# Block 0 of a cross-attention and expert layer: first loads on ScalarE's queue, row transposes ahead of values, squares of the expert weights regrouped

## The chip, the cores and the metric

The kernel runs on one core of a Trainium2 chip. The metric is the device time of one execution in microseconds (us), the median of several runs. Engines: TensorE (PE, with its weight loads PEld), VectorE (DVE), ScalarE (ACT), GpSimd (POOL) and SyncE (SP, which issues most transfers). A name with q behind it (SPq, ACTq) is the engine's sequencer, here when it issues a transfer.

## What is computed

```
x = x + attn(layernorm(x), ctx)   # 8 sequences of 256 tokens, 512 wide; 32 query heads of 16, 8 key/value groups
                                  #   q = ln(x) Wq', k = ctx Wk', v = ctx Wv', softmax(q k'/4) v, Wfc', + bfc
x = x + ffn(layernorm(x))         # 8 experts of width 352, top 2 of them within the 2 best of 4 groups,
                                  #   softmax gate, silu(g) * u, and a shared expert of width 704
```

All inputs are float32. The kernel splits float32 operands of its large products into two float16 parts (a high part and the rest), scaled by powers of two that it derives from maxima or sums of squares of the data, and takes three float16 products for one float32 product.

## The kernel before

The 2048 tokens are taken in four **blocks** of 512 tokens (`BLOCKS = 4`, `BT = 512`), each of four tiles of 128 tokens (`TPB = 4`). The first phase, to which the change belongs, ends about 103 us after the start. For each block n it computes keys (`project_k`, PE line 1087, 4 pairs of float32 matmuls into bank 0), values (`project_v(n, a)`, line 1092, one tile a at a time into bank 5), the transposed normalised rows (`x_transpose(n, a)`, line 1156, into four banks) and the queries (`project_q(n, m)`, line 1111, four groups m of 12 float16 matmuls). Later phases are attention (lines 1205, 1219, 1135 on PE, exponentials at ACT line 948), the output projection with the second layernorm, and the experts (PE lines 1377 and 1391).

Around these matmuls:

- **DVE** makes the layernorm of a block (`norm_block`, from line 1573 to 1586; for blocks 2 and 3 the last step, subtract and multiply, is POOL's, line 714), the largest absolute key (`k_top`, line 1600), the reduction of that over partitions (`top_of_all`, lines 1606 and 1608, between two small PE transposes, `top_transpose` at line 1120 and `top_back` at line 1124), the power-of-two scales (`top_scale`, lines 1614 to 1623), and the second float16 parts: of the transposed rows (`xT_rest`, line 1642), of the query weights (`wq_rest`, line 1658), of keys and queries (`cut_rest(n, l)`, line 1636; l = 0 is the keys, 1 to 4 the query groups). In blocks 2 and 3 it also reduces score maxima (line 1592) for fills that PE makes between halves of a query group.
- **ACT** makes the first float16 parts (`xT_first` line 883, `wq_first` line 889, `cut_first` line 861), copies the values out of their bank (`v_out`, line 895), takes the square root of a block's variance (`std_block`, line 866), squares the query weights to find their scale (line 901) and squares the gate and up weights of the ten expert matrices, in 20 halves (`square_half(h)`, line 871), each with its sum in one column.
- **SP** issues the loads and stores in one order. It loads block 0's rows (`load_x_block(0)`, line 408), then for each quarter k of the contraction the key/value weights and the context (lines 400 and 401), then the query weights in one transfer (line 418). It waits for the last quarter of the context, then issues rows and context of block 1, halves 0 and 1 of the expert weights (line 414), rows of block 2, and halves 2 and 3. In the loop over blocks it stores each pair of parts as soon as its second part is there (`store_parts`, line 432) and behind each store loads the half that is four further on (`load_half`), which waits until the half in that buffer has been squared. The parts are in three buffers, so `cut_first` number i waits until the store of number i - 3 has landed.

The order on each engine is written out by hand. In block 0 PE runs keys, three tiles of values, the transposes for both scales, the last tile of values, both `top_back`s, the four row transposes, then the queries. In blocks 1 to 3 it runs keys, row transposes, two tiles of values, then waits for the block's `k_top`, and goes on with `top_transpose`, two tiles of values, `top_back`, queries.

Of the kernel before, what the change touches and what calls it, by code (L numbers as in the profile page):

```python
# [31 lines left out]
D = 512  # L32
# [48 lines left out]
def build(nc, x, ctxT, wqT, wkvT, wfcT, bfc, gwT, wgu, wdn, out):  # L81
# [17 lines left out]
    with ExitStack() as ctx:  # L99
# [141 lines left out]
        def small(at, n):  # L241
# [10 lines left out]
        rstds, warm = [rstd[:], small(408, TPB)], small(416, TPB)  # L252
        WQ = BLOCKS
# [107 lines left out]
            sem("soft_in"), sem("soft_exp"), sem("sel_done"), sem("pre_ready"), sem("slots_done"), sem("offs_done"))  # L361
        iotas, hot_ready, table_ready, toks_done = sem("iotas"), sem("hot_ready"), sem("table_ready"), sem("toks_done")
# [12 lines left out]
        out_st, OUT_SEEN = x_ld + [w_q], (32, 16, 16, 16)  # L375
# [15 lines left out]
        def _(sp):  # L391
# [24 lines left out]
            load_x_block(0)  # L416
            load_ctx(0)
            sp.dma_start(wq_sb, wqT).then_inc(w_q, 16)
# [430 lines left out]
        def _(act):  # L849

            for stored in parts_st + lnt_stored:
                act.sem_inc(stored, FREE)
# [39 lines left out]
            def v_out(n):  # L892
# [7 lines left out]
            act.wait_ge(w_q, 16)  # L900
            nc.scalar.activation(wq_words, wq_sb.rearrange("p k n -> p (k n)"), ACT.Square,
                                 accum_out=kq_max[:, WQ:WQ + 1]).then_inc(wq_square, 1)
            for n in range(BLOCKS):
                if n == 0:
                    xT_first(0, 0)
                    act.wait_ge(kq_scaled, 1)
                    wq_first(0)
                    for a in range(1, TPB):
                        xT_first(0, a)
# [7 lines left out]
                if n == BLOCKS - 1:  # L917
                    neg_max_rows(0, 0, 0)
                if n < 2:
                    std_block(1 + n)  # L920
                square_half(KQ * n)
                for l in range(1, KQ):
                    cut_first(n, l)
                    if n < BLOCKS - 1:
                        square_half(KQ * n + l)
                    elif l < KQ - 1:
                        for h in ((16, 17), (18,), (19,))[l - 1]:
                            square_half(h)
# [122 lines left out]
            act.wait_ge(soft_in, 1)  # L1051
# [25 lines left out]
        def _(pe):  # L1077
# [82 lines left out]
            for n in range(BLOCKS):  # L1160
                last = n == BLOCKS - 1
                project_k(n)
                if n == 0:
                    for a in range(3):
                        project_v(n, a)
# [3 lines left out]
                    pe.wait_ge(kq_max_done, 1)  # L1169
                    top_transpose(0, bank[4])  # L1170
                    project_v(n, 3)
                    top_back(0, bank[3])
                    top_back(1, bank[4])
                    for a in range(TPB):
                        x_transpose(n, a)
                else:
# [6 lines left out]
                    project_v(n, 0)  # L1183
                    project_v(n, 1)
                    pe.wait_ge(kq_max_done, n + 1)
                    pe.wait_ge(rest_done, n * KQ + KQ)
                    top_transpose(n, bank[4])
                    project_v(n, 2)
                    project_v(n, 3)
                    top_back(n + 1, bank[4])  # L1190
                pe.wait_ge(xT_free, (n + 1) * TPB)
# [53 lines left out]
            pe.wait_ge(nm_in[0], 32)  # L1245
            for f in range(2):
                score_fill(0, f)
            for G in range(UNITS * UG):
# [12 lines left out]
                if G + 1 < UNITS * UG:  # L1261
                    if j == UG - 1:
                        pe.wait_ge(nm_in[(u + 1) % 4], (u + 1) // 4 * 32 + 32)
                    score_fill(G + 1, 0)
# [269 lines left out]
        def _(dve):  # L1534
# [110 lines left out]
            def neg_max_part(v, par, at=7):  # L1645
                dve.wait_ge(mxt_ready, v + 1)
                if v >= 2:
                    dve.wait_ge(nm_in[(v - 2) % 4], (v - 2) // 4 * 32 + 32)
# [13 lines left out]
            for n in range(BLOCKS):  # L1662
                v = n - 2
                k_top(n)
                if n == 0:
                    top_of_all(0, bank[3])
                    top_of_all(1, bank[4])
                    top_scale(0, WQ, bank[3])
                    top_scale(1, 0, bank[4])
                    exp_factor(0)  # L1670
                    xT_rest(0, 0)
                    wq_rest(0)
                    for a in range(1, TPB):
                        xT_rest(0, a)
                    wq_rest(1)
                    cut_rest(0, 0)
                    wq_rest(2)
                    wq_rest(3)
                else:
                    if n == BLOCKS - 1:  # L1680
                        neg_max_part(0, 0, at=3)
                    for a in range(TPB):
                        xT_rest(n, a)
                    top_of_all(n + 1, bank[4])
# [577 lines left out]
```

## Time and profile before

| | us |
|---|---|
| median of 3 runs | 849.8 (845.85 to 851.85) |
| the profiled execution, whole | 843.12 |
| its span, first to last instruction | 841.4 |
| PE busy in the span | 801.7 |
| DVE busy | 597.5 |
| ACT busy | 446.2 |
| POOL busy | 269.5 |
| mean granted TensorE clock | 0.991 of full |

The span is 1.7 us shorter than the execution's own time; the rest lies before the first and behind the last instruction. Busy shares are means over the whole kernel; the timeline rows further down show single stretches of it, with the start and the length of each group of instructions, and in brackets how long the engine had been idle before and what released it.

### The profile page before, as it was taken

How to read it: one execution, taken by the hardware profiler on the slowest of the kernel's cores; microseconds unless marked ns; L12 is line 12 of the kernel's file. 1: busy time of each engine (PE TensorE's matmuls, PEld its weight loads, DVE VectorE, ACT ScalarE, POOL GpSimd, SP SyncE). 2: the span in 40 equal slices, each digit the busy share in tenths (PEclk: the TensorE clock that was granted, in tenths of full speed). 3: DMA queues.
4: the chain of work that ended last, by engine and by line, in shares of the span. 5: the costliest groups of instructions: out<-in, count | busy, mean ns of one | idle time of the engine just before them, and what ended most of it. 6: DMA issues, size and time to landing. Idle time of an engine off the chain costs nothing.

```text
span 841.4 us, 17104 instructions
## 1 busy us (share of the span) xinstructions
PE 801.7 (95%) x5498; PEld 447.1 (53%) x5499; DVE 597.5 (71%) x1224; ACT 446.2 (53%) x876; POOL 269.5 (32%) x224
## 2 busy tenths in 40 slices
PE   5999999999999989999889999999999999999996
PEld 3553433333433346666545656666666666666663
DVE  4767789999999769896786665555555555546656
ACT  2665689999999835565335633333333333333332
POOL 2361029999953015661000111111111111032321
PEclk9999989999999999999999999999999999999999
DMA  8996755555457989976711222322322322156673
GB/s 314 365 363 216 229 196 181 162 191 189 156 149 229 324 300 326 372 248 219 282 51 63 88 85 78 97 78 75 100 75 77 97 75 82 56 177 202 186 212 125
DMA packets 68675, 149.08 MB, mean 177 GB/s; under 512 B 10704, under 2 KB 24528, under 8 KB 67984
## 3 DMA queue, kind: packets, MB, share of 16 engines
q1 hardware_dynamic: 57436, 106.99, 36.9%
q0 software_dynamic: 11120, 41.43, 15.9%
q8 instruction: 29, 0.48, 0.2%
q14 instruction: 22, 0.18, 0.1%
q10 hardware_dynamic: 68, 0.02, 0.0%
HBM read 105.40 MB, written 42.73 MB: 176 GB/s over the span
## 4 chain that ended last, share of the span: by engine, by line
PE 74%; DVE 12%; DMA 5%; ACT 5%; issue 3%; SPq 1%; DVEq 0%; ACTq 0%
PE psum L1377 26%; PE psum L1391 15%; PE psum L1219 8%; PE psum L1205 6%; PE psum L1135 4%; PE psum L1305 3%; PE psum L1367 3%; DMA sb_weights<-attn_dram 2%; PE psum L1111 2%; PE psum L1471 2%; PE psum L1236 2%; DMA sb_weights<-in_wdn 2%; DMA sb_weights<-in_wqT 1%; DVE sb_stats L1573 1%; DVE sb_rows L1592 1%
## 5 line engine op out<-in xcount | busy, mean ns | idle before, releaser
L1377 PE MATMUL psum<-sb_weights,sb_rows 128*128 (+1 forms) x1608 | 263.2, 314 | 0.6 <-issue 0.6
L1377 PEld LDWEIGHTS psum<-sb_weights,sb_rows 128*128 128x128 f16 x1608 | 157.5, 98 | 78.3 <-issue 0.8
L948 ACT ACTIVATE sb_weights<-psum,sb_rows 128x512 f32<-128x512 f32 x256 | 158.2, 684 | 16.9 <-PE psum L1205 15.0
L1391 PE MATMUL psum<-sb_weights,sb_hT 128*128 (+1 forms) x639 | 150.6, 381 | 4.7 <-DVE sb_hT L1853 4.7
L1592 DVE TENSOR_REDUCE sb_rows<-psum 128x4 f32<-128x1024 f32 x128 | 149.9, 1214 | 4.3 <-PE psum L1135 4.3
L825 POOL DMA_INDIRECT sb_rows<-xn_rows,sb_slot_tok x39 | 38.1, 978 | 267.8 <-PE psum L1471 204.9
L1018 ACT ACTIVATE psum<-sb_h 128x352 f32<-128x352 f32 x71 | 33.2, 468 | 144.4 <-DVE sb_h L1835 144.4
L1391 PEld LDWEIGHTS psum<-sb_weights,sb_hT 128*128 128x128 f16 x639 | 62.0, 98 | 72.9 <-DVE sb_hT L1853 7.3
L1030 ACT CAST sb_hT<-psum 128x384 f16<-128x384 f32 x71 | 33.9, 478 | 113.6 <-PE psum L1367 113.2
L1205 PE MATMUL psum<-sb_weights 50*128 50x512 f16 x256 | 90.1, 391 | 3.0 <-ACT sb_weights L948 2.6
L1853 DVE TENSOR_TENSOR sb_hT<-psum,sb_hT 128x384 f16<-128x384 f32 x71 | 39.3, 554 | 72.5 <-ACT sb_hT L1030 72.5
L1219 PE MATMUL psum<-sb_weights 128*32 128x256 f32 x1024 | 82.9, 396 | 0.0
L1135 PE MATMUL psum<-sb_weights 48*128 48x256 f16 x512 | 73.0, 275 | 0.8 <-DVE sb_rows L1592 0.8
L1305 PE MATMUL psum<-sb_weights 128*128 128x512 f32 x128 | 57.7, 594 | 0.3 <-ACT sb_weights L958 0.3
L843 POOL DMA_INDIRECT sb_weights<-slot_y,sb_p_i x32 | 32.2, 1005 | 80.3 <-DMA out<-sb_weights 42.5
L1205 PEld LDWEIGHTS psum<-sb_weights 50*128 50x128 f16 x256 | 23.6, 93 | 63.3 <-ACT sb_weights L948 59.1
L1023 ACT ACTIVATE sb_h<-sb_h,sb_h_scale_i 128x352 f32<-128x352 f32 x71 | 41.8, 588 | 15.7 <-DVE sb_h_scale_i L1841 15.7
L1111 PE MATMUL psum<-sb_weights 128*128 128x512 f16 x192 | 44.6, 380 | 2.9 <-DVE sb_weights L1642 2.9
L734 POOL TENSOR_TENSOR sb_weights<-sb_weights,sb_w_scale_i 128x1408 f32<-128x1408 f32 x15 | 38.5, 2570 | 26.6 <-ACT sb_weights L990 25.8
L1841 DVE TENSOR_SCALAR sb_h_scale_i<-sb_h_sum 128x1 int32<-128x1 int32 x71 | 10.9, 154 | 46.7 <-ACT psum L1018 46.7
L744 POOL TENSOR_TENSOR sb_weights<-sb_weights 128x1408 f16<-128x1408 f32 x15 | 43.0, 2864 | 1.2
L1367 PE MATMUL psum<-sb_ident,sb_h 128*128 128x128 f32 x213 | 35.6, 277 | 2.5 <-ACT sb_h L1023 2.3
(254 smaller groups left out, 1126.5 us busy)
## 6 DMA issues: line engine op xcount, KB each, us to landing
sb_weights<-in_wgu SPq DMA_DIRECT2D x20, 704.0 KB, 6.1
sb_weights<-in_wgu POOLq DMA_DIRECT2D x20, 704.0 KB, 5.5
sb_weights<-in_wdn SPq DMA_DIRECT2D x17, 768.0 KB, 6.4
slot_y<-sb_rows SPq DMA_DIRECT2D x39, 256.0 KB, 2.0
sb_weights<-q_parts SPq DMA_DIRECT2D x96, 64.0 KB, 2.3
x_dram<-sb_rows SPq DMA_DIRECT2D x24, 256.0 KB, 2.5
sb_weights<-in_x SPq DMA_DIRECT2D x4, 1024.0 KB, 7.5
q_parts<-sb_weights SPq DMA_DIRECT2D x16, 256.0 KB, 4.4
```

Of the source, the lines that this page charges most:

```text
L744: nc.gpsimd.tensor_tensor(low, stage, high, ALU.subtract).then_inc(gu_cut, 1)
L948: nc.scalar.activation(probs[G % 2][:, kt, pair * 512:(pair + 1) * 512], bank[4 + f % 2], ACT.Exp, scale=exp_scale[:, n:n + 1]).then_inc(e ...
L1023: nc.scalar.activation(h_sb[par][:, 0:F], h_sb[par][:, 0:F], ACT.Copy, scale=h_scale[:, par:par + 1]).then_inc(h_done, 1)
L1111: mm = nc.tensor.matmul(bank[Q_BANKS[n][m]], wq16[:, wp, k, m * P:(m + 1) * P], xnT[n % 2][:, xp, k, :], start=(k == 0 and i == 0), stop=( ...
L1135: mm = nc.tensor.matmul(bank[banks[qt] + side][:, h * SEQ:(h + 1) * SEQ], q_st[s][lo:hi, g, h, b * SEQ + qt * P:b * SEQ + (qt + 1) * P], k ...
L1205: nc.tensor.matmul(bank[4 + side].rearrange("p (h t) -> p h t", h=HH), k_st[s][lo:hi, g, b * SEQ + kt * P:b * SEQ + (kt + 1) * P], q_st[s] ...
L1219: mm = nc.tensor.matmul(bank[6][VW * c:VW * (c + 1), 0:SEQ], v_now, probs[G % 2][:, kt, c * SEQ:(c + 1) * SEQ], start=(kt == 0), stop=(kt ...
L1305: mm = nc.tensor.matmul(bank[2 + s][:], oT[s][:, k, :], wfc_sb[:, k, :], start=(k == 0), stop=(k == KD - 1))
L1367: tr = nc.tensor.transpose(bank[HT_BANK][:, j * P:(j + 1) * P], h_sb[par][:, j * P:(j + 1) * P], ident[:])
L1377: mm = nc.tensor.matmul(bank[GU_BANKS[par][which]][:, 0:F], x_T[:, xp * D + k * P:xp * D + (k + 1) * P], gu(wp, k, which), start=(k == 0 a ...
L1391: mm = nc.tensor.matmul(bank[Y_BANKS[par]][:], hT[par][:, hp, j, :], dn(wp, j), start=(j == 0 and n == 0), stop=(j == NF - 1 and n == 2))
L1592: nc.vector.tensor_reduce(to[:, :, j // UB, :, j % UB, qt], psum[:, banks[qt] * 512:(banks[qt] + 2) * 512] .rearrange("p (a h k) -> p a h ...
```

## The change

Three things change, all of them in the first phase.

1. ACT issues block 0's rows as its first instruction and behind them the query weights in four transfers of 256 KB, one per quarter of the contraction. SP starts with the context and no longer issues these. The query weights are squared quarter by quarter, each with its own sum in one column of `wq_squares`, and DVE adds the four sums.
2. In block 0 PE makes the row transposes ahead of the values. `k_top(0)` and the scale of the keys come behind the scale of the query weights on DVE. In all blocks PE now waits for `k_top` before any values, then runs `top_transpose`, two tiles of values, `top_back` (in block 0 behind the fourth tile), two tiles of values. DVE takes `top_of_all` ahead of the block's last `xT_rest`.
3. The 20 squares of the expert weights are grouped (2, 1, 1, 1, 0) per block: two behind the keys' first part and ahead of the next block's square root, one behind each of the next three `cut_first`, none behind the last.

Some waits on shared semaphores get an offset, because two semaphores serve a second purpose.

```diff
@@ SP
-            load_x_block(0)
             load_ctx(0)
-            sp.dma_start(wq_sb, wqT).then_inc(w_q, 16)
             sp.wait_ge(c_first[KD - 1], 32)
@@ ACT
+            act.dma_start(x_in[0], x_blocks[0]).then_inc(x_ld[0], 16)
+            for k in range(KD):
+                act.dma_start(wq_sb[:, k, :], wqT[:, k, :]).then_inc(wq_ld[k], 16)
...
             std_block(0)
-            act.wait_ge(w_q, 16)
-            nc.scalar.activation(wq_words, wq_sb.rearrange("p k n -> p (k n)"), ACT.Square,
-                                 accum_out=kq_max[:, WQ:WQ + 1]).then_inc(wq_square, 1)
+            for k in range(KD):
+                act.wait_ge(wq_ld[k], 16)
+                nc.scalar.activation(wq_words[:, k * D:(k + 1) * D], wq_sb[:, k, :], ACT.Square,
+                                     accum_out=wq_squares[:, k:k + 1]).then_inc(wq_squared, 1)
+            SQUARES = (2, 1, 1, 1, 0)
             for n in range(BLOCKS):
                 if n == 0:
-                    xT_first(0, 0)
+                    for a in range(2):
+                        xT_first(0, a)
                     act.wait_ge(kq_scaled, 1)
                     wq_first(0)
-                    for a in range(1, TPB):
+                    for a in range(2, TPB):
                         xT_first(0, a)
...
+                for h in range(SQUARES[0]):
+                    square_half(KQ * n + h)
                 if n < 2:
                     std_block(1 + n)
-                square_half(KQ * n)
                 for l in range(1, KQ):
                     cut_first(n, l)
-                    if n < BLOCKS - 1:
-                        square_half(KQ * n + l)
-                    elif l < KQ - 1:
-                        for h in ((16, 17), (18,), (19,))[l - 1]:
-                            square_half(h)
+                    for h in range(sum(SQUARES[:l]), sum(SQUARES[:l + 1])):
+                        square_half(KQ * n + h)
@@ PE
                 project_k(n)
                 if n == 0:
-                    for a in range(3):
-                        project_v(n, a)
                     pe.wait_ge(consts, 2)
                     pe.wait_ge(wq_square, 1)
                     top_transpose(WQ, bank[3])
-                    pe.wait_ge(kq_max_done, 1)
-                    top_transpose(0, bank[4])
-                    project_v(n, 3)
+                    for a in range(2):
+                        x_transpose(0, a)
                     top_back(0, bank[3])
-                    top_back(1, bank[4])
-                    for a in range(TPB):
-                        x_transpose(n, a)
+                    for a in range(2, TPB):
+                        x_transpose(0, a)
                 else:
...
                     pe.wait_ge(v_free, n + 1)
-                    project_v(n, 0)
-                    project_v(n, 1)
-                    pe.wait_ge(kq_max_done, n + 1)
                     pe.wait_ge(rest_done, n * KQ + KQ)
-                    top_transpose(n, bank[4])
-                    project_v(n, 2)
-                    project_v(n, 3)
+                pe.wait_ge(kq_max_done, n + 1)
+                top_transpose(n, bank[4])
+                project_v(n, 0)
+                project_v(n, 1)
+                if n > 0:
                     top_back(n + 1, bank[4])
+                project_v(n, 2)
+                project_v(n, 3)
+                if n == 0:
+                    top_back(1, bank[4])
@@ DVE
-                k_top(n)
                 if n == 0:
+                    dve.wait_ge(wq_squared, KD)
+                    nc.vector.tensor_reduce(kq_max[:, WQ:WQ + 1], wq_squares, AX.X, ALU.add).then_inc(wq_square, 1)
+                    k_top(0)
                     top_of_all(0, bank[3])
-                    top_of_all(1, bank[4])
                     top_scale(0, WQ, bank[3])
-                    top_scale(1, 0, bank[4])
-                    exp_factor(0)
                     xT_rest(0, 0)
                     wq_rest(0)
                     for a in range(1, TPB):
                         xT_rest(0, a)
+                    top_of_all(1, bank[4])
                     wq_rest(1)
+                    top_scale(1, 0, bank[4])
+                    exp_factor(0)
                     cut_rest(0, 0)
                     wq_rest(2)
                     wq_rest(3)
                 else:
+                    k_top(n)
...
-                    for a in range(TPB):
+                    for a in range(3):
                         xT_rest(n, a)
                     top_of_all(n + 1, bank[4])
+                    xT_rest(n, 3)
```

## Rows read from the trace of the kernel before

**Rows 1.** The page: busy time (us, share, instructions), and shares of the last chain

```profile
PE 801.7 (95%) x5498; PEld 447.1 (53%) x5499; DVE 597.5 (71%) x1224; ACT 446.2 (53%) x876; POOL 269.5 (32%) x224
...
PE 74%; DVE 12%; DMA 5%; ACT 5%; issue 3%; SPq 1%; DVEq 0%; ACTq 0%
```

**Rows 2.** Stretches of 3 us: busy us by engine, clock, DMA share, GB/s

```profile
3.00:6.00 3.00, 0.00 (x0) 0.00 (x0) 0.00 (x0) 0.15 (x1) 2.88 (x5) 1.00 1.05 376
...
33.00:36.00 3.00, 3.00 (x9) 1.43 (x8) 1.40 (x3) 3.00 (x5) 2.84 (x4) 1.00 0.86 281
...
63.00:66.00 3.00, 1.44 (x11) 0.97 (x10) 2.59 (x9) 1.18 (x3) 3.00 (x2) 1.00 1.01 385
```

**Rows 3.** Timeline, block 0: start, length, engine, line, operation, idle before

```profile
0.81 0.46 SPq L408 DMA_DIRECT2D sb_weights<-in_x  x1
...
6.10 2.47 DVE L1573 BATCH_NORM_STATS2 sb_stats<-sb_weights 128x6 f32<-128x512 f32 x4 [6.10 <-DMA sb_weights<-in_x]
...
9.23 0.21 ACT L866 ACTIVATE sb_std<-sb_var_e 128x4 f32<-128x4 f32 x1 [6.08 <-DVE sb_var_e L1579]
...
10.47 1.92 DVE L1586 TENSOR_SCALAR sb_weights<-sb_weights,sb_mv,sb_rstd 128x512 f32<-128x512 f32 x4
...
11.77 0.38 SPq L408 DMA_DIRECT2D sb_weights<-in_x  x1
...
14.23 1.91 ACT L901 ACTIVATE sb_weights<-sb_weights 128x2048 f32<-128x2048 f32 x1 [4.80 <-DMA sb_weights<-in_wqT]
...
16.05 0.19 ACT L901 ACTIVATION_READ_ACCUMULATOR sb_weights<-sb_weights 128x1 f32 x1
...
17.84 0.16 DVE L1614 TENSOR_SCALAR sb_rows<-psum 128x1 f32<-128x1 f32 x1 [0.17 <-PE psum L1124]
...
22.75 10.54 PE L1111 MATMUL psum<-sb_weights 128*128 128x512 f16 x48 [2.91 <-DVE sb_weights L1642]
...
26.14 2.46 DVE L1573 BATCH_NORM_STATS2 sb_stats<-sb_weights 128x6 f32<-128x512 f32 x4
```

**Rows 4.** Timeline, head of block 1, columns as in rows 3

```profile
37.49 0.60 ACT L861 ACTIVATE sb_weights<-psum 128x512 f16<-128x512 f32 x1 [1.15 <-DMA q_parts<-sb_weights]
37.99 1.37 ACT L871 ACTIVATE sb_weights<-sb_weights 128x1408 f32<-128x1408 f32 x1
...
38.73 0.68 DVE L1600 TENSOR_REDUCE sb_rows<-psum 128x1 f32<-128x512 f32 x1
...
39.97 2.48 DVE L1642 SCALAR_TENSOR_TENSOR sb_weights<-psum,sb_weights 128x512 f16<-128x512 f32 x4 [0.55 <-ACT sb_weights L883]
...
40.19 1.95 PE L1092 MATMUL psum<-sb_weights 128*128 128x128 f32 x16
...
43.09 3.20 PE L1111 MATMUL psum<-sb_weights 128*128 128x512 f16 x14
```

**Rows 5.** Timeline, end of block 1 and head of block 2, same columns

```profile
53.04 2.46 DVE L1573 BATCH_NORM_STATS2 sb_stats<-sb_weights 128x6 f32<-128x512 f32 x4
...
62.16 2.48 DVE L1642 SCALAR_TENSOR_TENSOR sb_weights<-psum,sb_weights 128x512 f16<-128x512 f32 x4 [0.56 <-ACT sb_weights L883]
...
65.43 1.47 PE L1111 MATMUL psum<-sb_weights 128*128 128x512 f16 x6
```

**Rows 6.** Timeline, head of block 3, same columns

```profile
87.00 1.95 PE L1092 MATMUL psum<-sb_weights 128*128 128x128 f32 x16
...
89.03 1.47 PE L1111 MATMUL psum<-sb_weights 128*128 128x512 f16 x6
...
89.87 0.69 ACT L861 ACTIVATE sb_weights<-psum,sb_rows 128x512 f16<-128x512 f32 x1 [0.30 <-DVEq L1624]
```

**Rows 7.** Stretches of 1 us at attention's start, columns as in rows 2

```profile
104.00:105.00 1.00, 0.26 (x1) 0.09 (x1) 1.00 (x2) 1.00 (x2) 0.00 (x0) 1.00 0.34 98
...
106.00:107.00 1.00, 1.00 (x6) 0.30 (x5) 0.38 (x1) 1.00 (x2) 0.00 (x0) 0.62 0.33 103
...
112.00:113.00 1.00, 1.00 (x8) 0.37 (x6) 0.27 (x1) 0.24 (x1) 0.00 (x0) 0.50 0.30 74
```

More of the change, by code:

```diff
@@ L252, in build @@
         rstds, warm = [rstd[:], small(408, TPB)], small(416, TPB)
+        wq_squares = small(420, KD)
         WQ = BLOCKS
@@ L361, in build @@
             sem("soft_in"), sem("soft_exp"), sem("sel_done"), sem("pre_ready"), sem("slots_done"), sem("offs_done"))
+        wq_ld, NM_SEEN = nm_in, 16
+        wq_squared, SOFT_SEEN = soft_in, KD
         iotas, hot_ready, table_ready, toks_done = sem("iotas"), sem("hot_ready"), sem("table_ready"), sem("toks_done")
@@ L374, in build @@
         out_done = sem("out_done")
-        out_st, OUT_SEEN = x_ld + [w_q], (32, 16, 16, 16)
+        out_st, OUT_SEEN = x_ld + [w_q], (32, 16, 16, 0)
         B0, C0 = PA, PA + PB
@@ L1049, in _ @@
             hidden_scale(1, 1)
-            act.wait_ge(soft_in, 1)
+            act.wait_ge(soft_in, 1 + SOFT_SEEN)
             nc.scalar.activation(score, score, ACT.Exp).then_inc(soft_exp, 1)
@@ L1244, in _ @@
             pe.wait_ge(v_free, BLOCKS + 1)
-            pe.wait_ge(nm_in[0], 32)
+            pe.wait_ge(nm_in[0], 32 + NM_SEEN)
             for f in range(2):
@@ L1262, in _ @@
                     if j == UG - 1:
-                        pe.wait_ge(nm_in[(u + 1) % 4], (u + 1) // 4 * 32 + 32)
+                        pe.wait_ge(nm_in[(u + 1) % 4], (u + 1) // 4 * 32 + (32 + NM_SEEN))
                     score_fill(G + 1, 0)
@@ L1647, in neg_max_part @@
                 if v >= 2:
-                    dve.wait_ge(nm_in[(v - 2) % 4], (v - 2) // 4 * 32 + 32)
+                    dve.wait_ge(nm_in[(v - 2) % 4], (v - 2) // 4 * 32 + (32 + NM_SEEN))
                 nc.vector.tensor_scalar(nm[par][:, 0, :], bank[at][0:NM, MXT:MXT + P], -1.0 / ONE, None,
```

## The prediction

> **What bounds the kernel now.** I read the page first: PE is busy for 95% of the span and carries 74% of the chain that ended last [rows 1]. That share is a mean; the change touches only the first phase, about 105 of 841 us, so the question is what sets the pace there. The table by stretches of 3 us says that PE is far from full in places: in 63 to 66 it works 1.44 of 3 us. It says too that the DMA engines are full (share 1.00 and more) from 3 us on and still are at 63 to 66, with dips such as 0.86 at 33 to 36 [rows 2]. Then I read the timeline for the head of each block, because there PE changes from one kind of matmul to the next through a chain over ACT and DVE.
>
> Block 0 [rows 3]: the rows, issued at 0.81, land at 6.10; the last context quarter has landed at 11.77 (SP's next load is released then); the query weights are there at 14.23, and their square is read out by 16.24. The first scale is read by DVE at 17.84, PE starts queries at 22.75, and DVE reaches block 1's layernorm at 26.14. Block 1 [rows 4]: DVE's `k_top` stands at 38.73, the first `xT_rest` at 39.97, queries start at 43.09. Block 2 [rows 5]: 62.16 and 65.43. Block 3 [rows 6]: queries at 89.03, straight behind the values; PE alone sets it.
>
> **The loads.** The same 3.67 MB (rows 1.05, key/value weights 0.52, context 1.05, query weights 1.05) go over DMA engines that are already full [rows 2]. A second issuer brings them no bandwidth, so the last of them lands at about 14.2 as before, and what is gained by ACT issuing query weights early is taken from the context or the rows. The sum takes nothing here. The rows now share with context from the start. Their landing is bounded by 6.1 (as if alone) and 11.8 (together with all context) [rows 3]; no row shows the sharing, so I take the middle, 8.9. In its own sentences: the Trainium skill, "DMA: Bandwidth & Descriptors", section "Queues, rings and completion order", says that each DMA engine goes round between the queues packet by packet. By that rule 1.05 MB of context pass beside the rows, 2.8 us at 376 GB/s, and the rows land at 8.9; were the queues served in order of issue they would land at 6.1, and the end would come out about 0.1 us earlier than below, since then the last quarter of the weights bounds the squares. No row of the kernel before has two such queues side by side, so the trace neither agrees nor disagrees.
>
> **The squares of the query weights.** ACT takes the root first. The root now starts 3.13 us behind the rows' landing (9.23 less 6.10) and takes 0.21 [rows 3]: 8.9 + 3.3 = 12.2. A square of 2048 columns takes 1.91 and one of 1408 takes 1.37 [rows 3, 4], 0.84 ns a column, so 512 columns take 0.61, and 0.19 for each read-out: 0.80. Four of them: 12.2 + 3.2 = 15.4 (or 14.2 + 0.8 = 15.0, if the last quarter bounds). DVE adds the four sums, about 0.2; its layernorm is done by then (8.9 + 6.29 = 15.2, from 6.10 to 12.39). At 15.65 `k_top(0)`, which used to be hidden, stands in the chain with 0.68 [rows 4]; then the reduction over partitions and the way through PE, 0.65 (43.09 less 42.45, where the block 1 chain does the same) [rows 4]. The first scale is read at 17.0 instead of 17.84: **0.8 us gained**.
>
> **From there to block 1.** Before, DVE took 8.30 us from the first scale to the next layernorm [rows 3]. Now the keys' scale comes after all `xT_rest` and one `wq_rest`; `cut_first(0, 0)` on ACT (0.7) can't start before it and used to be covered by DVE's other work, and `wq_rest(0)` waits about 0.25 for a first part that itself waits for the scale. I add 1.0: 9.3, so layernorm 1 starts at 26.3 (+0.15). The gain of 0.8 is spent. PE's order lets values (four tiles, 3.9 by [rows 4]) run under DVE's parts; queries start behind DVE's scale and its five second parts (4.35 us), `top_of_all` and `top_back` (0.95 together), at 17.0 + 5.3 = 22.3, 0.45 earlier, and this has no taker, because PE then waits for DVE in block 1. SP: two ahead of one, halves 4 and 5 are asked for some 4 us earlier; the engines are full, so what is in the queue ahead of a store stays about the same. The store that releases `cut_first(0, 4)` at 37.49 [rows 4] is issued behind DVE's layernorm 1, and I leave it there (+0.1). The bound upward: half 4 lands so late that its square, now ahead of `cut_first(0, 4)`, pushes it by up to 0.8.
>
> **Head of block 1 (the term that costs).** What the regrouping frees: ACT's square of 1.37 and its 0.19 no longer stand between `cut_first(0, 4)` and `xT_first(1, 0)`. DVE idled 0.55 for it [rows 4]. That is the gain, 0.5, since `k_top` and `cut_rest` keep DVE busy anyway. What the wait costs: PE now stands until `k_top` is done (39.4 to 39.6) and only then starts values that it had made from about 38.2 on (two tiles ahead of 40.19), under `k_top`. From there: `top_transpose` 0.25, two tiles 1.95 [rows 4], `top_back` 0.35 to 0.5 later (three `xT_rest` and `top_of_all` are 2.4 to 2.5), two tiles 1.95: 4.65 us from `k_top`'s end to queries, against 43.09 less 39.41 = 3.68 before. Queries start at 39.6 + 4.65 = 44.25, **1.15 later** than before. Behind that wait on PE stand the values, `top_back` and the queries; behind the values stands `v_out` on ACT, and behind it `cut_first(1, 0)`, so layernorm 2 starts some 0.9 later.
>
> **Block 2.** The regrouping gives part of that back in block 1: the squares fall into ACT's idle time ahead of the root, so ACT is late by 0.1 to 0.2 at layernorm 3 (53.2 against 53.04 [rows 5]), not by 0.9. The last `cut_first` stands where it was, and DVE's idle 0.56 ahead of the first `xT_rest` (62.16) [rows 5] goes: `k_top` ends at about 61.75. Plus 4.65: queries at 66.4 against 65.43, 1.0 later, of which 0.75 reaches the second fill, since the keys' scale is ready earlier.
>
> **Block 3.** All is shifted by 0.75. The head is PE's own work [rows 6] and `k_top` has been long done, so the reordering costs nothing; its cover is DVE's idle time. The keys' scale, on which ACT waited 0.30 at 89.87 [rows 6], is ready before: 0.25 back. **Sum: +1.15 and +1.0 are not added, the second contains the first; +0.75 - 0.25 = +0.5 us** at the start of attention, and behind it everything starts by the same semaphores. The profiled execution goes from 843.1 to 843.6; the median of 849.8 is 6.7 above that execution, so I forecast 850.3.
>
> **Rivals.**
> *The gain arrives.* If DVE gets its first scale earlier and the wait on `k_top` hides (values finish before `top_back` anyway), the 0.8 of the head and 0.5 of each of two heads come through: -1.8, so 848.0. For it: DVE's two idle gaps are real [rows 4, 5]. Against: 1.95 us of values lose their cover in two blocks.
> *Rows late.* This one ends slower than before. Layernorm 0 ends 6.29 behind the rows. From a landing at 9.4 on, it and not the squares sets the first scale, and each further us costs one. With the context (11.8) that is 2.4, with the last weights (14.2) 4.8: 852.7 to 855.1. For it: the DMA engines are full [rows 2]. Against: the rows are first in ACT's queue.
> *A colder clock.* At 104 to 105 PE is busy for 0.26 of 1 us; the granted clock is 0.62 at 106 to 107 and 0.50, that is 1.2 GHz, until 113 [rows 7]: 6.6 us at half, 3.3 lost where PE sets the pace. The longer wait at the heads of blocks 1 and 2 could bring the same there, 853.6; or the shift could spare the one at 106, 847. Against: in block 0, PE stands 2.91 us before 22.75 [rows 3], longer than any new wait, with full clock behind it. In sentences of its own: the Trainium skill, "TensorE: Matmul & The Clock Gate", Part 1, says that the clock is halved after idle time and returns after sustained work, and that when this falls varies from run to run. By it the fall after 104 fits, while block 0's wait without one doesn't show it; it gives the same 853.6.
> *It does nothing.* Full DMA engines pin the landings on which the heads wait; 849.8. It differs from my forecast by less than can be measured.
>
> **How the numbers follow.** Forecast 0.45 (its own range 849 to 852), the gain arrives 0.2, rows late 0.12, clock 0.08, nothing 0.15. The runs of before lie 4 below to 2 above their median, which is wider than most of these terms, and about 1% (8.5 us) is what a measurement of this kernel can tell from no change. Low end: 848.0 less 3.5; high end: 855.1 plus 1. Over 1% faster would need 8.5 us in a phase where PE's summed waits at the heads are smaller: 0.03. Over 1% slower needs late rows and a fallen clock together: 0.04.
>
> **What would show it.** Right: first scale read near 17.0; layernorm 1 within 0.5 of 26.14; no idle DVE between `k_top(1)` and the first `xT_rest`; `k_top`'s end to queries 4.65 in blocks 1 and 2; block 3 unchanged but for the earlier `cut_first`; attention starting 0.5 later. Wrong: the rows landing past 9.4, the context's last quarter much past 11.8 (it holds back block 1's loads), `cut_first(0, 4)` behind half 4's landing, or a granted clock of 0.5 before 100 us.

## The result and the profile after

| | before | changed |
|---|---|---|
| median of 20 runs, us | 848.7 (843.9 to 853.7) | 852.6 (848.6 to 855.4) |
| ratio, 95% interval | | 1.0042 (1.0024 to 1.0060) |
| profiled execution, span | 841.4 | 846.8 |
| first exponential of attention, us after the start | 104.0 | 106.35 |

The changed kernel is slower by 0.4%, some 3.6 us. I had forecast +0.5 us. The first exponential (ACT) marks the end of the phase that was changed; up to there the profiled execution has lost 2.35 us. The timeline of the changed kernel, columns as in rows 3; these rows answer to those of [rows 3]:

```profile
7.18 2.47 DVE L1577 BATCH_NORM_STATS2 sb_stats<-sb_weights 128x6 f32<-128x512 f32 x4 [7.18 <-DMA sb_weights<-in_x]
...
11.99 5.28 PE L1092 MATMUL psum<-sb_weights 128*128 128x512 f32 x6 [1.52 <-DMA sb_weights<-in_ctxT]
...
14.70 0.16 DVE L1670 TENSOR_REDUCE sb_rows<-sb_rows 128x1 f32<-128x4 f32 x1 [1.23 <-ACT sb_weights L906]
...
15.09 0.39 SPq L411 DMA_DIRECT2D sb_weights<-in_x  x1
...
17.30 0.69 DVE L1604 TENSOR_REDUCE sb_rows<-psum 128x1 f32<-128x512 f32 x1 [2.45 <-PE psum L1092]
...
18.74 0.16 DVE L1618 TENSOR_SCALAR sb_rows<-psum 128x1 f32<-128x1 f32 x1 [0.31 <-PE psum L1129]
...
23.56 10.53 PE L1116 MATMUL psum<-sb_weights 128*128 128x512 f16 x48
...
27.46 2.47 DVE L1577 BATCH_NORM_STATS2 sb_stats<-sb_weights 128x6 f32<-128x512 f32 x4
```

The rows land at 7.18 (6.10 before). The query weights are squared and summed at 14.86, against 16.24 before: that part does what it says. But the context's last quarter lands at 15.09 instead of 11.77 (SP's next load of rows is released by it). PE's keys end at 17.3 (line 1092 is `project_k` in the changed kernel), `k_top(0)` (line 1604) waits 2.45 for them, and the first scale is read at 18.74, 0.9 later than before, not 0.8 earlier. The table by stretches of 2 us (columns as in rows 2) shows a second effect. First the kernel before:

```profile
12.00:14.00 2.00, 2.00 (x14) 1.52 (x14) 1.08 (x2) 0.00 (x0) 0.00 (x0) 1.00 0.67 229
14.00:16.00 2.00, 1.60 (x15) 1.41 (x13) 0.00 (x0) 1.77 (x1) 0.00 (x0) 1.00 1.07 407
16.00:18.00 2.00, 1.62 (x13) 1.49 (x14) 1.07 (x5) 0.23 (x2) 0.00 (x0) 1.00 1.01 380
```

Then the changed kernel, in which the DMA engines stand still (share 0.07) just where they used to be full:

```profile
12.00:14.00 2.00, 2.00 (x2) 0.49 (x2) 1.47 (x4) 1.15 (x5) 0.00 (x0) 1.00 0.68 256
14.00:16.00 2.00, 1.90 (x3) 0.84 (x3) 0.16 (x1) 0.67 (x2) 0.00 (x0) 1.00 0.07 26
16.00:18.00 2.00, 2.00 (x12) 1.31 (x10) 0.69 (x2) 0.15 (x1) 0.00 (x0) 1.00 0.68 224
```

Before, the query weights were behind the context in the one queue and kept the engines busy while SP waited for the context and issued the next loads. Now both queues drain together, and nothing is queued until SP is released at 15.09. The next loads in SP's queue are asked for about 3 us later, and at the head of block 1 ACT runs late behind transfers (ACT's timeline; compare [rows 4]):

```profile
37.20 0.60 ACT L865 ACTIVATE sb_weights<-psum 128x512 f16<-128x512 f32 x1 [1.70 <-DMA k_parts<-sb_weights]
38.84 1.38 ACT L875 ACTIVATE sb_weights<-sb_weights 128x1408 f32<-128x1408 f32 x1 [1.04 <-DMA sb_weights<-in_wgu]
...
40.21 0.58 ACT L865 ACTIVATE sb_weights<-psum 128x512 f16<-128x512 f32 x1
40.69 2.05 ACT L887 ACTIVATE sb_weights<-psum 128x512 f16<-128x512 f32 x4
```

A `cut_first` waits 1.70 for the store of the keys' parts (issued at 26.25, landed 10.9 us later, behind the loads), the square behind it 1.04 for half 4, and `cut_first(0, 4)` comes at 40.21 instead of 37.49. The two waits themselves are not made by the late context: they stand in e2 below too, nearly as long, but 2.9 us earlier. Queries of block 1 start at 46.43 (43.09 before), of block 2 at 68.30 (65.43), of block 3 at 91.53 (89.03).

### The profile page after: what moved, and what is told of

Read it like the earlier page. It is cut to its first block, busy times and chain, and to the rows that moved or that the text cites. A ratio compares the mean times of both kernels' runs of the same rounds, so it can differ in the third digit from the quotient of the medians.

```text
span 846.8 us, 17114 instructions
## 1 busy us (share of the span) xinstructions
PE 802.4 (95%) x5498; PEld 446.7 (53%) x5499; DVE 597.0 (71%) x1225; ACT 447.8 (53%) x882; POOL 269.4 (32%) x224
## 3 DMA queue, kind: packets, MB, share of 16 engines
q0 software_dynamic: 11120, 41.43, 15.5%
## 4 chain that ended last, share of the span: by engine, by line
PE 74%; DVE 11%; DMA 6%; ACT 4%; issue 3%; SPq 1%; another core or an unknown queue 0%; ACTq 0%; DVEq 0%
PE psum L1381 26%; PE psum L1395 14%; PE psum L1223 7%; PE psum L1209 6%; PE psum L1140 4%; PE psum L1309 4%; PE psum L1116 3%; PE psum L1371 3%; PE psum L1475 2%; PE psum L1240 2%; DMA sb_weights<-in_wdn 2%; DMA sb_weights<-attn_dram 2%; DMA sb_weights<-in_wgu 1%; DMA sb_weights<-in_ctxT 1%; PE psum L1097 1%
## 5 line engine op out<-in xcount | busy, mean ns | idle before, releaser
L953 ACT ACTIVATE sb_weights<-psum,sb_rows 128x512 f32<-128x512 f32 x256 | 158.5, 684 | 17.0 <-PE psum L1209 15.1
L1861 DVE TENSOR_TENSOR sb_hT<-psum,sb_hT 128x384 f16<-128x384 f32 x71 | 39.3, 554 | 70.8 <-ACT sb_hT L1035 68.3
L1849 DVE TENSOR_SCALAR sb_h_scale_i<-sb_h_sum 128x1 int32<-128x1 int32 x71 | 10.9, 154 | 46.7 <-ACT psum L1023 46.7
```

The costliest lines, as they stand in the source:

```text
L953: nc.scalar.activation(probs[G % 2][:, kt, pair * 512:(pair + 1) * 512], bank[4 + f % 2], ACT.Exp, scale=exp_scale[:, n:n + 1]).then_inc(e ...
```

## The experiments

"First exp" is the first exponential in the profiled execution; it moves by what the first phase gains or loses, and nothing behind that phase blurs it. It is still the mark of a single execution: two kernels were traced twice, and their marks differ by 0.8 (e11 and e12) and 1.2 us (changed and e13, where the clock fell once in the second). So a difference of 2 us between two rows is clear of this spread, and tenths are not. Each ratio is against runs of the kernel before on the same chip, with its 95% interval.

| kernel | context's last quarter | queries of blocks 1, 2, 3 start | first exp | ratio |
|---|---|---|---|---|
| before | 11.8 | 43.1, 65.4, 89.0 | 104.00 | |
| changed | 15.1 | 46.4, 68.3, 91.5 | 106.35 | 1.0042 (1.0024 to 1.0060) |
| e1 loads only | 15.0 | 48.0, 70.3, 93.9 | 108.86 | 1.0027 (0.9999 to 1.0056) |
| e2 changed, loads back | 11.9 | 43.5, 66.0, 89.3 | 104.09 | 0.9991 (0.9961 to 1.0021) |
| e3 changed, SP doesn't wait | | 43.7, 67.1, 90.6 | 105.45 | 0.9994 (0.9970 to 1.0018) |
| e4 squares only | 11.9 | 43.9, 64.5, 87.8 | 102.77 | 0.9987 (0.9955 to 1.0018) |
| e5 later blocks' order only | 11.8 | 43.7, 67.8, 91.4 | 106.20 | 1.0011 (0.9979 to 1.0042) |
| e6 changed, that order back | 15.0 | 45.1, 65.5, 89.1 | 104.07 | 0.9997 (0.9973 to 1.0022) |
| e7 loads and order back | 11.8 | 42.2, 63.7, 86.8 | 101.79 | 0.9970 (0.9938 to 1.0001) |
| e8 as e7, SP doesn't wait | | 41.5, 63.7, 88.4 | 103.38 | 0.9956 (0.9925 to 0.9988) |
| e10 changed, only the rows on ACT | 10.8 | 42.3, 64.5, 87.9 | 102.72 | 0.9996 (0.9963 to 1.0029) |
| e11 as e10, order back | 10.7 | 40.6, 62.0, 85.2 | 100.13 | 0.9898 (0.9861 to 0.9936) |
| e12, e11 again | 10.5 | 40.8, 62.4, 86.0 | 100.95 | 0.9959 (0.9933 to 0.9986) |
| e13, changed again | 15.1 | 47.8, 69.5, 92.8 | 107.59 | 1.0051 (1.0027 to 1.0074) |

**e1, the loads alone.** The kernel before with the loads and the quartered square (the square's lines are left out here):

```diff
-            load_x_block(0)
             load_ctx(0)
-            sp.dma_start(wq_sb, wqT).then_inc(w_q, 16)
...
+            act.dma_start(x_in[0], x_blocks[0]).then_inc(x_ld[0], 16)
+            for k in range(KD):
+                act.dma_start(wq_sb[:, k, :], wqT[:, k, :]).then_inc(wq_ld[k], 16)
```

> The kernel before with only the loads and the quartered square of the query weights taken over (ACT issues block 0's rows and the query weights); the orders on PE and the grouping of the expert squares stay. Theory A (the hole in the transfers): the context's last quarter lands near 15.1 instead of 11.8, the next loads are issued 3.3 us later and the DMA engines idle between 13 and 17; queries of block 1 start at 45 to 46 instead of 43.1, the first exponential comes at 105.5 to 106.5 instead of 104.0, time +1.5 to +2.5 us. Theory B (PE's wait on the largest key costs, the loads don't): first exponential at 104 +- 0.3, time unchanged.

The context is late as in the changed kernel, and the phase loses 4.9 us, more than expected. The granted clock was 0.52 and 0.62 from 28 to 32 in this execution, in the middle of block 0's queries, so a part of the 4.9 may be that. But 4.05 us were already lost at the first scale (21.89 against 17.84), before the clock fell: in the old order of block 0 three tiles of values stand on PE between the keys and the transposes for both scales, so late keys push the first scale by more than in the changed kernel. A loss from the loads is shown; for the changed kernel its size is better read from the pairs below.

**e2, the changed kernel with the loads back on SP** (query weights in quarters behind the context).

```diff
+            load_x_block(0)
             load_ctx(0)
+            for k in range(KD):
+                sp.dma_start(wq_sb[:, k, :], wqT[:, k, :]).then_inc(wq_ld[k], 16)
...
-            act.dma_start(x_in[0], x_blocks[0]).then_inc(x_ld[0], 16)
-            for k in range(KD):
-                act.dma_start(wq_sb[:, k, :], wqT[:, k, :]).then_inc(wq_ld[k], 16)
```

> The changed kernel with its loads on SP again in the old order (rows, context, query weights, the last still in quarters); the new orders and the new grouping stay. Theory A: the context has landed at 11.8, no idle DMA engines, queries of block 1 near 44.2, first exponential at 104.3 to 104.8, time near +0.5 us over the kernel before. Theory B: the head of block 1 still costs 2 us and more, first exponential near 106.

Its timeline, DVE and SP, then ACT at the head of block 1:

```profile
11.94 0.38 SPq L411 DMA_DIRECT2D sb_weights<-in_x  x1
...
15.39 0.68 DVE L1604 TENSOR_REDUCE sb_rows<-psum 128x1 f32<-128x512 f32 x1
...
16.95 0.16 DVE L1618 TENSOR_SCALAR sb_rows<-psum 128x1 f32<-128x1 f32 x1 [0.44 <-PE psum L1129]
...
34.31 0.60 ACT L865 ACTIVATE sb_weights<-psum 128x512 f16<-128x512 f32 x1 [1.63 <-DMA k_parts<-sb_weights]
35.92 1.38 ACT L875 ACTIVATE sb_weights<-sb_weights 128x1408 f32<-128x1408 f32 x1 [1.02 <-DMA sb_weights<-in_wgu]
...
37.30 0.58 ACT L865 ACTIVATE sb_weights<-psum 128x512 f16<-128x512 f32 x1
```

The context is there at 11.94 and the first scale at 16.95, where I had put 17.0. The first exponential comes at 104.09, a little ahead of the 104.3 to 104.8 expected. Theory A holds: with the loads back 2.26 of the 2.35 us are gone, and block 1's queries come 2.9 us earlier (43.52 against 46.43). ACT waits here as in the changed kernel, for the store of the keys' parts and for half 4, which is thus what the new grouping brings with it (e4, with the grouping alone, has both waits, 0.70 and 1.02); `cut_first(0, 4)` comes behind them at 37.30, no later than the 37.49 of the kernel before.

**e3, SP doesn't wait for the context** ahead of block 1's loads.

```diff
-            sp.wait_ge(c_first[KD - 1], 32)
             load_x_block(1)
```

> The changed kernel without SP's wait for the context's last quarter ahead of block 1's loads. Theory A in its narrow form (the hole between 13 and 17 us is made by this wait): DMA engines busy throughout, block 1's rows and the halves land 3 us earlier, the store that releases the fourth and fifth first part lands earlier, first exponential at 104.5 to 105.3. Rival within A: the late context itself delays the first scale (18.7), and the hole is harmless: first exponential stays near 106.

The hole is gone (share 1.05 and more from 12 to 18 us) and queries of block 1 start at 43.7, 2.7 earlier. The first scale is later still (19.35): the late context is not mended by it. Yet `k_top(1)` starts at 38.64, as in e2 (38.52), and not at 41.43. So in block 1 of the changed kernel it was the late transfers that cost, and a first scale as late as that cost next to nothing. (In e3 block 1's rows are asked for at 5.12, even earlier than in e2, so the two are not otherwise alike.) At the first exponential (105.45, just outside the 104.5 to 105.3 expected) only 0.9 is left of the 2.7. The trace shows one reason; in the table by stretches of 2 us PE idles at the head of block 2, behind its wait on `k_top(2)`, and then the clock is at half:

```profile
60.00:62.00 2.00, 0.48 (x5) 0.51 (x6) 1.92 (x4) 2.00 (x5) 2.00 (x2) 1.00 1.04 175
62.00:64.00 2.00, 2.00 (x15) 2.00 (x13) 1.97 (x5) 0.00 (x1) 2.00 (x2) 0.65 1.08 323
64.00:66.00 2.00, 2.00 (x10) 1.76 (x10) 1.03 (x6) 0.00 (x0) 2.00 (x2) 0.50 1.02 371
```

**e4, only the squares regrouped.**

```diff
+                for h in range(SQUARES[0]):
+                    square_half(KQ * n + h)
                 if n < 2:
                     std_block(1 + n)
-                square_half(KQ * n)
                 for l in range(1, KQ):
                     cut_first(n, l)
-                    if n < BLOCKS - 1:
-                        square_half(KQ * n + l)
...
+                    for h in range(sum(SQUARES[:l]), sum(SQUARES[:l + 1])):
+                        square_half(KQ * n + h)
```

> The kernel before with only the squares of the expert weights grouped (2, 1, 1, 1, 0). Theory: ACT is free for the row parts at the head of block 1, DVE's 0.55 us of idle time goes, queries of block 1 start 0.4 to 0.6 earlier (42.5 to 42.7) and the first exponential comes 0.5 to 1.2 earlier (102.8 to 103.5); time -0.5 to -1.2 us. Rival: half 4 is not there yet and its square holds up the last first part of block 0: queries of block 1 no earlier than 43.1, no gain.

1.2 us earlier at the first exponential, the upper end of what was expected. Queries of block 1 start 0.8 later, not earlier: this execution had the clock at 0.68 and 0.50 from 22 to 26, in block 0's queries, and its keys of block 1 start 1.7 later (34.82). By block 2 it is 1.0 ahead. The gain is shown, its place in block 1 is not.

**e5, only the new order of blocks 1 to 3** on PE and DVE (the edit below, on the kernel before), and **e6, the changed kernel with that order taken back**.

```diff
+                    pe.wait_ge(rest_done, n * KQ + KQ)
+                    pe.wait_ge(kq_max_done, n + 1)
+                    top_transpose(n, bank[4])
                     project_v(n, 0)
                     project_v(n, 1)
-                    pe.wait_ge(kq_max_done, n + 1)
-                    pe.wait_ge(rest_done, n * KQ + KQ)
-                    top_transpose(n, bank[4])
+                    top_back(n + 1, bank[4])
                     project_v(n, 2)
                     project_v(n, 3)
-                    top_back(n + 1, bank[4])
...
-                    for a in range(TPB):
+                    for a in range(3):
                         xT_rest(n, a)
                     top_of_all(n + 1, bank[4])
+                    xT_rest(n, 3)
```

> The kernel before with only the new order of PE and DVE in blocks 1 to 3 (wait for the largest key ahead of all values). Theory B: from the end of the largest key to the queries it takes 4.3 to 4.65 us instead of 3.68 in blocks 1 and 2, so queries of block 1 start at 43.7 to 44.1 instead of 43.09, of block 2 0.5 to 1.0 later, of block 3 the same amount less 0.3; first exponential at 104.2 to 104.8, time +0.2 to +0.8 us. Rival: other work hides the wait, all within 0.2 of the kernel before.

> The changed kernel with the old order of PE and DVE in blocks 1 to 3; the loads on ACT stay. Theory A (the loads are the main cost, the later blocks' order the smaller): context's last quarter still at 15.1, queries of block 1 about 1 us earlier than in the changed kernel (45.4 instead of 46.4), first exponential 1 to 1.6 earlier (104.8 to 105.4 instead of 106.35), so still behind the kernel before (104.0). Theory B (the order is what costs): first exponential at 103 to 104, all of the loss gone.

e5 loses 0.6 in block 1, which looks as expected, but its `k_top(1)` ended 0.7 earlier than before (38.70 against 39.41): from there to the queries it takes 4.97, more than the 4.3 to 4.65 expected. In all it loses 2.2, more than expected; here too the clock was at 0.56 and 0.59 from 62 to 66, behind PE's wait in block 2. e6 gives back 2.28, more than the 1 to 1.6 expected, with the context still late. Its 104.07 is nearer to what theory B gave than to theory A's: the order costs as much as the loads do. Its timeline at the head of block 1:

```profile
39.14 1.95 PE L1097 MATMUL psum<-sb_weights 128*128 128x128 f32 x16
...
41.40 0.68 DVE L1604 TENSOR_REDUCE sb_rows<-psum 128x1 f32<-128x512 f32 x1
42.23 0.27 PE L1125 MATMUL psum<-sb_ident,sb_rows 128*1 128x128 f32 x1 [1.13 <-DVE sb_rows L1604]
42.34 1.95 PE L1097 MATMUL psum<-sb_weights 128*128 128x128 f32 x16
...
45.11 1.25 PE L1116 MATMUL psum<-sb_weights 128*128 128x512 f16 x5
```

Two tiles of values (39.14) are made ahead of `k_top`'s end (42.08), and queries follow it by 3.03 us; in the changed kernel by 4.32.

**e7, both taken back.** What is left of the change is block 0's order, the quartered square and the grouping.

> The changed kernel with the loads back on SP and the old order of blocks 1 to 3; what stays of the change is block 0's order, the quartered square of the query weights and the new grouping. If the loads and the later blocks' order are the two parts that cost, this one beats the kernel before: queries of block 1 at 42.6 to 43, first exponential at 102.5 to 103.3 (104.0 before), time -1 us. Rival: block 0's order costs as much as the grouping gains, first exponential at 103.8 to 104.2.

It beats the kernel before by 2.2 us at the first exponential, more than the 0.7 to 1.5 expected. With e2 and e6 it completes a table of four, all with the rest of the change in:

| first exponential | new order in blocks 1 to 3 | old order |
|---|---|---|
| loads on ACT | 106.35 | 104.07 |
| loads on SP | 104.09 | 101.79 |

Either step costs 2.3 us, with or without the other. In none of the four executions did the clock fall ahead of the mark. That the pairs agree to 0.02 is luck, given the 0.8 by which a repeat differed; e10 with e11 and e12 below gives 2.6 and 1.8 for the order. The rest of the change gains 2.2, of which e4 shows some 1.2 for the grouping; block 0's order was never run alone, so its share is not shown.

**e8, e7 without SP's wait.**

```diff
-            sp.wait_ge(c_first[KD - 1], 32)
             load_x_block(1)
```

> As the run before it, and SP does not wait for the context ahead of block 1's loads. With one queue the wait made only a short dip in the DMA share (0.63 and 0.70 between 12 and 14 us), so taking it away moves block 1's loads by 0.5 us at most: first exponential within 0.5 of the run before it. Rival: the loads of block 1 take bandwidth from the query weights, first scale later by 1 us and more.

1.6 later than e7 at the first exponential, where 0.5 at most was expected, all of it lost between the queries of blocks 2 (63.7 in both) and 3 (88.4 against 86.8); in this execution the granted clock was 0.74, 0.50 and 0.91 in the three stretches of 2 us from 64 to 70. The rival's mark, a first scale later by 1 us, is not there (17.17 against 16.81 in e7). Whether the early loads harm otherwise stays open.

**e10, only the rows on ACT**, and **e11 and e12, the same with the old order in blocks 1 to 3**.

```diff
             load_ctx(0)
+            for k in range(KD):
+                sp.dma_start(wq_sb[:, k, :], wqT[:, k, :]).then_inc(wq_ld[k], 16)
...
             act.dma_start(x_in[0], x_blocks[0]).then_inc(x_ld[0], 16)
-            for k in range(KD):
-                act.dma_start(wq_sb[:, k, :], wqT[:, k, :]).then_inc(wq_ld[k], 16)
```

> The changed kernel where ACT issues only block 0's rows; the query weights stay behind the context in SP's queue. If it is the query weights that delay the context, its last quarter is there at 11.5 to 12.5 again, no idle DMA engines behind it, and the first exponential comes at 104 to 104.6 as with all loads on SP. Rival: the rows alone delay it (they are as many bytes), the context lands at 13 or later and the first exponential at 105 or later.

> The candidate: ACT issues block 0's rows, the query weights stay behind the context on SP in quarters; old order in blocks 1 to 3; block 0's order and the grouping (2, 1, 1, 1, 0) of the change. From the two runs with one of these each: context at 10.8, queries of block 1 at 41.2 to 41.8, first exponential at 101.3 to 102.2 (104.0 before), time -2 to -3.5 us, ratio 0.996 to 0.998. Rival: in block 1 the landing of the stores bounds now, and it is no better than the run with all loads on SP (101.8).

> The candidate once more, beside the changed kernel on the same chip. Its first phase is 3.9 us shorter than that of the kernel before, which is 0.46% of the whole; the ratio of 0.990 measured first is larger than that. Theory: the first phase is all that it gains, ratio 0.993 to 0.998, first exponential at 100 to 101.5. Rival: something behind the first phase gains too, ratio again 0.988 to 0.992.

e10 and the changed kernel differ only in the place of the query weights. With the rows alone on ACT the context's last quarter lands at 10.8, earlier than the 11.5 to 12.5 expected, a microsecond earlier than before and 4.3 earlier than in the changed kernel. The DMA engines have no hole (e10, by stretches of 2 us):

```profile
12.00:14.00 2.00, 0.89 (x3) 0.06 (x1) 1.33 (x3) 2.00 (x8) 0.00 (x0) 1.00 0.98 345
14.00:16.00 2.00, 1.50 (x12) 1.35 (x13) 1.31 (x5) 0.92 (x4) 0.00 (x0) 1.00 1.03 407
```

The first exponential comes at 102.72, and with the old order at 100.13 and 100.95: 3.9 and 3.0 ahead of the kernel before. The kernel of e11 and e12, called the candidate in their expectations, ran at 0.9898 and 0.9959 of the time of the kernel before. It is faster than both kernels (839.5 against 847.4 for the changed and 843.9 for the kernel before on one chip). The second ratio is what 3 to 4 us of 845 make; the first is more, rests on 7 runs, and the repeat did not show it again.

**e13, the changed kernel again.**

> The changed kernel once more. Theory: first exponential at 106 to 107 with the context's last quarter at 15 us again and the DMA engines idle between 14 and 17; the stall of 3 us near 755 us in its first trace is no part of the change and is absent; ratio 1.002 to 1.006.

Context at 15.06, hole and loss as before, ratio 1.0051. Its first exponential (107.59) is 1.2 later than the first time and outside the 106 to 107 expected; the clock was at half from 43 to 46. The first trace had a stall near 755 us, in the last expert units: PE was busy for 16.78 of 20 us,

```profile
740.00:760.00 20.00, 16.78 (x101) 9.71 (x99) 6.47 (x17) 5.92 (x14) 7.58 (x8) 1.00 0.58 188
```

and is full there in this one:

```profile
740.00:760.00 20.00, 20.00 (x128) 12.49 (x126) 9.12 (x25) 7.38 (x18) 4.09 (x5) 1.00 0.41 141
```

So some 3 of the 5.4 us by which the two first spans differ are no part of the change.

## Why the prediction was right or wrong

The range held the time, and no change beyond 1% was the likely case. But the range, 844.5 to 856.1, is 11.6 us wide, and 852.6 lies just outside the 849 to 852 that I gave the forecast itself. The direction was right and the size was not: +3.6 us against +0.5. One term of the sum had been put at nothing, and two others, a cost and a gain, were both too small and cancelled, which was luck.

**The loads: wrong, and this is the step that failed.** I wrote that what ACT's queue gains "is taken from the context or the rows", and then: "The sum takes nothing here." The first half was right. The second left out that PE and SP wait for the context. Its last quarter came 3.3 us later; that cost 2.26 us (106.35 against 104.09). It made the first scale late (18.74 against 16.95 in e2) and the next loads late, and e3 shows that in block 1 it was the loads that counted. How the 2.26 at the end of the phase divides between the two stays open, since e3's clock fell in block 2. The mistake was to look at when the last of the 3.67 MB lands instead of at which transfer a chain waits for. Even that landing was wrong: I had put it at 14.2 as before, and it was 15.1, because the last to land was now the context itself. I had named the sign of it ("much past 11.8 (it holds back block 1's loads)") and given it no price and no rival. The rival of late rows was the wrong one: they landed at 7.18, within the bounds 6.1 to 11.8 and 1.7 earlier than the 8.9 that I took, and never set the first scale. That the time came out at the rival's 852.7 is chance.

**The first scale: the number right in e2, partly by luck.** 17.0 was forecast and 16.95 is what e2 has, but e2 is not the case that I had summed. Its rows landed at 6.29 and not at 8.9, and its first square waited for its quarter of the weights until 12.62 (the sum had 12.2, from the rows). The squares then followed each other every 0.65 us and not every 0.80, because the read-out overlaps the end of its square; [rows 3] already showed this, with 14.23 + 1.91 + 0.19 = 16.33 against a read-out that ended at 16.24. And from the start of `k_top(0)` to the first scale it took 1.56, not 1.33. In the changed kernel the squares wait for their quarters instead (0.52, 0.38 and 0.48 ahead of the last three). In e2 the layernorm of block 1 starts at 25.7, against 26.3 forecast and 26.14 before: I had spent 0.6 too much between.

**The wait on `k_top`: mechanism right, sum wrong.** From its end to the queries: 4.32 in block 1 and 4.81 in block 2 of the changed kernel, 4.65 forecast, 3.68 and 3.82 before. But I wrote that the two losses "are not added, the second contains the first". They are added: e2 is 1.3 us behind e7 at block 1's queries (43.52 against 42.20) and 2.35 behind at block 2's (66.04 against 63.69). In all the wait costs 2.28 to 2.30 in the two pairs.

**The grouping: right, larger.** DVE no longer idles between `k_top(1)` and the first `xT_rest`, as forecast. The sign that I had named against it, `cut_first(0, 4)` behind half 4's landing, came too, but did no harm against the kernel before where the loads are on SP (37.30 in e2). I gave the grouping 0.5 in each of two heads and 0.25 in block 3; e4 gained 1.2. With block 0's order the gain is 2.2 (e7). The two errors, wait and gain both too small, cancel: without the loads, +0.5 was forecast and +0.09 measured.

**The rivals.** *The gain arrives* (-1.8) is what e7 does (-2.2), once the two costs are out. *A colder clock*: it did not fall in the changed kernel's first profile before 100 us, but in e1, e3, e4, e5, e8 and e13 it did, in different places.

**Open.** 2.35 us are 0.28% of the whole; the measured 0.42% (0.24 to 0.60) leaves room for something behind the first phase that I have not traced. The whole times agree in direction with the marks: without the new place of the loads (e2, 0.9991) or without the new order (e6, 0.9997) the loss is gone. Their intervals are too wide to give the size.

## What to carry to other kernels

When the DMA engines are full, a second queue adds little or no bandwidth: from 2 to 11 us they moved 334 GB/s before, 340 in e10 and 300 in the changed kernel. It changes who is served first. Put on it what is needed first, and leave in the first queue, behind what a chain waits for, whatever is needed last; a late bulk transfer there also keeps the engines busy while the issuing engine waits. Price each wait that such a shift touches, with the landing of its own transfer and not that of the last. Where an engine is made to wait earlier in its order, the cost is the work that used to run under that wait.

## What the runs showed of the hardware

**Two queues.** Rows and query weights on ACT, context on SP: with the same issue times of the context within 0.4 us, the context's last quarter lands at 15.1 with 2.1 MB on the other queue and at 10.8 with 1.05 MB on it. The Trainium skill, "DMA: Bandwidth & Descriptors", section "Queues, rings and completion order", says that each DMA engine takes the queues in turn packet by packet, and a whole packet at a time. That this gives both queues an even share was my own estimate from it, and put the rows at 8.9. They landed at 7.02 to 7.18 in eight runs, with more than an even share: in all eight only ACT's queue (q10) moved data from 3 to 5 us, though the first quarter of the context had been issued on SP's (q1) at 1.26. The DMA queues of the changed kernel from 3 to 5 us, then from 5 to 7 us (packets, MB, share of 16 engines):

```profile
q10 hardware_dynamic: 311, 0.64, 97.2%
```

```profile
q10 hardware_dynamic: 212, 0.40, 59.3%
q1 hardware_dynamic: 138, 0.26, 35.7%
```

From 5 us on both queues were served, as the page has it; from 3 to 5 the trace shows no turn for SP's. In e10 the context caught up once the rows had landed. In the changed kernel the query weights, behind the rows in ACT's queue, kept it back: from 7 to 11 us ACT's queue moved 0.69 MB and SP's 0.48.

**The clock at attention's start.** PE has gaps there in every run, and only in some the granted clock falls to half. From the first exponential to the end of the last it took 189.2 to 189.9 us in the six runs in which the clock stood at half for about 7 us there (the kernel before, the changed kernel twice, e4, e8 and e11), 188.3 to 188.8 in three in which it did for about half as long (e2, e5 and e10), and 187.2 to 187.6 in the five without a fall (e1, e3, e6, e7 and e12). Here, the kernel before and then e7:

```profile
106.00:110.00 4.00, 4.00 (x29) 1.23 (x28) 2.64 (x5) 2.70 (x5) 0.00 (x0) 0.53 0.59 189
```

```profile
106.00:110.00 4.00, 3.83 (x38) 1.24 (x38) 3.46 (x7) 3.82 (x8) 0.00 (x0) 1.00 0.34 113
```

About 2 us, 0.25% of the kernel, go with the longer fall, which is as much as the steps that were tested. That, beside stalls like the one at 755 us, is part of why whole times spread by some us here, and why the phases had to be compared by marks in the trace.
